# Expert layer: one region of rows per expert for the whole input, and finished tiles added to the result by an accumulating indirect DMA

## The reference

```python
# attention layer: Q, gate from layernorm(x); K, V from ctx (4 x 1024 x 512)
out = attn * gate @ Wo.T
x = x + out
# expert layer, on h = layernorm(x)
logits = einsum("bsd,de->bse", h, Wr)          # 8 experts
w, sel = top_k(logits, 2);  w = softmax(w)     # 2 experts per token, weights w
for e in range(8):
    out = out + gate[..., e:e+1] * (einsum("bsd,df->bsf", h, We[e]) + be[e])
x = x + out
```

## Time and profile before

| | us |
|---|---|
| median of three runs | 607.82 (605.88 to 607.92) |
| the profiled execution | 602.09 |
| its span, first to last instruction | 600.6 |
| TensorE busy in it | 546.1 |

### The profile page before, as it was taken

How to read it: one execution, slowest core, us unless ns; L and a number is a source line. 1 busy time by engine, 2 the same in 40 slices (tenths; PEclk the granted TensorE clock), 3 DMA queues, 4 the chain that set the end, 5 groups by cost and what they waited for, 6 DMA issues and landing times.

```text
span 600.6 us, 12872 instructions
## 1 busy us (share of the span) xinstructions
PE 546.1 (91%) x4192; PEld 443.6 (74%) x4193; DVE 320.0 (53%) x857; ACT 186.9 (31%) x340; POOL 166.9 (28%) x194
## 2 busy tenths in 40 slices
PE   6999996999999999999999999994899999999850
PEld 4778785788878888877888887883678888877630
DVE  4463374356436727535746645770566544447744
ACT  5456321334532343443244343231111111111100
POOL 3014645403633131554040350010112000055413
PEclk9999999799999999999999999996899999999995
DMA  8813344632453062355052137789847568789946
GB/s 270 308 37 106 141 141 169 201 122 108 149 196 114 18 229 71 139 179 207 4 202 80 72 141 297 264 286 420 306 147 241 145 206 269 226 254 369 408 178 189
DMA packets 44446, 114.18 MB, mean 190 GB/s; under 512 B 4976, under 2 KB 4976, under 8 KB 43504
## 3 DMA queue, kind: packets, MB, share of 16 engines
q1 hardware_dynamic: 24240, 57.43, 28.6%
q0 software_dynamic: 11232, 39.85, 18.5%
q10 hardware_dynamic: 8928, 16.26, 7.1%
HBM read 66.86 MB, written 46.66 MB: 189 GB/s over the span
## 4 chain that ended last, share of the span: by engine, by line
PE 61%; DMA 12%; issue 5%; POOL 3%; SPq 3%; DVE 3%; ACT 1%; POOLq 0%; DVEq 0%; ACTq 0%
PE pj L1098 17%; PE pj L1100 17%; PE pj L1099 17%; DMA khat<-xs 5%; PE tp L1090 4%; PE tp L1165 3%; DMA out_dram<-wraw 1%; DMA wraw<-in_L_ffn_We_dram 1%; POOL aux L533 1%; PE pj L1185 1%; PE kvb L1157 1%; DMA we_halves<-aux 1%; PE pj L1107 1%; DMA qhat<-y,gidx 1%; SPq L365 1%
## 5 line engine op out<-in xcount | busy, mean ns | idle before, releaser
L1098 PE MATMUL pj<-R 128*128 128x512 f32 x448 | 185.6, 414 | 10.3 <-DVE R L806 9.3
L1100 PE MATMUL pj<-R 128*128 128x512 f32 x448 | 177.4, 396 | 0.0
L1099 PE MATMUL pj<-R 128*128 128x512 f32 x448 | 176.8, 395 | 0.0
L1098 PEld LDWEIGHTS pj<-R 128*128 128x128 f32 x448 | 85.4, 191 | 27.4 <-DVE R L806 10.3
L1100 PEld LDWEIGHTS pj<-R 128*128 128x128 f32 x448 | 85.2, 190 | 19.3
L1099 PEld LDWEIGHTS pj<-R 128*128 128x128 f32 x448 | 85.7, 191 | 15.4
L1098 PE MATMUL pj<-R,aux 128*128 x184 | 77.5, 421 | 5.5 <-issue 3.6
L1100 PE MATMUL pj<-R,aux 128*128 x184 | 73.2, 398 | 0.0
L1099 PE MATMUL pj<-R,aux 128*128 x184 | 73.0, 397 | 0.0
L716 ACT CAST aux<-tp 128x512 fp32r<-128x512 f32 x46 | 26.9, 585 | 121.6 <-PE tp L1165 114.5
L806 DVE TENSOR_TENSOR R<-tp,R 128x512 fp32r<-128x512 f32 x64 | 43.8, 684 | 24.9 <-ACT R L638 24.7
(11 more groups left out here) (158 smaller groups left out, 652.5 us busy)
## 6 DMA issues: line engine op xcount, KB each, us to landing
we_halves<-aux POOLq DMA_DIRECT2D x14, 1024.0 KB, 5.0
R<-we_halves SPq DMA_DIRECT2D x7, 2048.0 KB, 11.9
khat<-xs SPq DMA_DIRECT2D x46, 256.0 KB, 3.6
wraw<-in_L_ffn_We_dram POOLq DMA_DIRECT2D x16, 512.0 KB, 6.4
buf<-in_ctx_dram SPq DMA_DIRECT2D x15, 512.0 KB, 3.8
y<-kvbd ACTq DMA_DIRECT2D x23, 256.0 KB, 3.6
y<-zeros ACTq DMA_DIRECT2D x23, 256.0 KB
wraw<-in_x_dram SPq DMA_DIRECT2D x4, 1024.0 KB, 8.0
```

Of the source, the lines that this page charges most:

```text
L1098: nc.tensor.matmul(bank[:, :], s_hi(k), m_hi(k), start=(k == 0), stop=False)
L1099: nc.tensor.matmul(bank[:, :], s_hi(k), m_lo(k), start=False, stop=False)
L1100: last = nc.tensor.matmul(bank[:, :], s_lo(k), m_hi(k), start=False, stop=(k == KT - 1))
```

## The change

There is one region of rows per expert for all four batches, and 39 tiles instead of 46. The first 17 are taken from the full tiles that the first three batches already give (`plan_full`), the other 22 from what is left when batch 3 is ranked (`plan_rest`). Each row in `xs` is 528 wide instead of 512: behind the normed row stand the token's weight for each expert, its number and a mark for rows that pad a tile. Rows and bias results have four buffers each instead of two.

A finished tile no longer goes to `y`. VectorE picks the weight and the number of each row's token (`pay`), adds the bias (`copy_y`), ScalarE multiplies by the weight (`scale_y`), and GpSimd adds the 128 rows to the result in device memory with one indirect DMA that accumulates (`add_rows`). Two tiles can hold the same token, and `add_rows(m)` waits until the add of tile m - 1 has landed. x2 is stored straight into the result. A pad row adds to the row of a token that is not otherwise in the tile; which one is worked out from the first 256 tokens (`mark_pads`, `find_pads`). The gathers, the combining on VectorE, the stores to `y` and of the result, and the loading of x2 are gone. All tiles stand in `START`, without loops.

The core of the diff:

```diff
-    GROUP_TILES = ((B - 1) * TT, TT)
-    ROWS = [n * P + P for n in GROUP_TILES]
...
+    ROWS = B * L + P
+    PAIRS = 2 * B * L
+    M0 = (2 * (B - 1) * L - E * (P - 1) + P - 1) // P
+    M_ALL = PAIRS // P + E - 1
+    M1 = M_ALL - M0
+    STEPS = B * L // P
...
+    XS, YS = 4, 4
...
+        for m in range(9, M_ALL):
+            START += tiles(m) + ([("C", "", 0)] if m == M0 - 2 else [])
+        START.remove(("T", "m", M_ALL))
...
+            def load_tile(m):
+
+                row = sp.value_load(tile_row[0:1, m:m + 1], min_val=0, max_val=E * ROWS)
+                if m >= XS:
+                    sp.wait_ge(MOE["t_m"], mth(m - XS))
+                    sp.wait_ge(paid, m - XS + 1)
+                sp.dma_start(xs_raw[:, m % XS, :], xs_dram[bass.ds(row, P), :]).then_inc(xs_loaded[m % XS], 16)
...
+                sp.wait_ge(wx_stored, 16 * 2 * e)
...
+            sp.wait_ge(SEMS["k"], nth("k", B - 1, ST - 1))
+            load_halves(1)
+            sp.wait_ge(SEMS["v"], nth("v", B - 1, ST - 1))
+            load_halves(2)
             sp.wait_ge(wx_stored, 16 * 2 * (E - 1))
-            sp.wait_ge(SEMS["v"], nth("v", B - 1, ST - 1))
-            load_halves(1)
-            load_halves(2)
+            sp.dma_start(be_all[:, 0:4, :], be[0:4, :].rearrange("(a e) d -> a e d", a=1).broadcast_to((P, 4, D))).then_inc(be_loaded, 16)
             sp.wait_ge(SEMS["q"], nth("q", B - 1, G - 1))
             load_halves(3)
+            sp.wait_ge(zeroed, 1)
+            sp.dma_start(xs_dram[E * ROWS:E * ROWS + P, :], zeros[:, :]).then_inc(padded, 16)
             sp.wait_ge(planned, 1)
-            sp.wait_ge(zeroed, 1)
-            with sp.Fori(0, E) as e:
-                pad(0, e, zeros[:, :])
-            sp.wait_ge(padded[0], 16 * E)
             for t in range(TT):
                 sp.wait_ge(scattered[t], 32 * (B - 1))
-            load_tile(0, 0, 0)
-            load_tile(0, 1, 1)
-            sp.wait_ge(SEMS["qhat"], nth("qhat", B - 1, G - 1))
-            for e in range(E):
-                sp.dma_start(be_all[:, e, :], be[e:e + 1, :].broadcast_to((P, D))).then_inc(be_loaded, 16)
+            for m in range(XS):
+                load_tile(m)
             sp.wait_ge(SEMS["g"], nth("g", B - 1, TT - 1))
             load_halves(4)
             load_halves(5)
-            load_tile(0, 2, 0)
+            load_tile(XS)
+            store_x2(B - 1)
             sp.wait_ge(SEMS["wo"], nth("wo", B - 1, TT - 1))
-            load_tile(0, 3, 1)
             load_halves(6)
-            load_tile(0, 4, 0)
+            load_tile(XS + 1)
             load_halves(7)
-            sp.wait_ge(x2_stored, 16 * B)
-            sp.wait_ge(SEMS["x2"], nth("x2", B - 1, TT - 1))
-            load_x2r(4, 4, x2r_loaded[1])
-            with sp.Fori(1, PAIRS - 4) as h:
-                load_tile(0, 2 * h + 3, 1)
-                load_tile(0, 2 * h + 4, 0)
+            for m in range(XS + 2, 14):
+                load_tile(m)
             sp.wait_ge(planned, 2)
-            sp.wait_ge(zeroed, 2)
-            for m in range(FIRST[1] - E, FIRST[1]):
-                load_tile(0, m, m % 2)
-                e = m - (FIRST[1] - E)
-                pad(1, e, bias[:, :])
-                if e >= 4:
-                    load_x2r(e - 4, 1, x2r_loaded[0])
-            sp.wait_ge(padded[1], 16 * E)
+            for e in range(E):
+                row = sp.value_load(pad_row[0:1, e:e + 1], min_val=0, max_val=E * ROWS - P)
+                sp.dma_start(xs_dram[bass.ds(row, P), :], zeros[:, :]).then_inc(padded, 16)
+            for m in range(14, M0):
+                load_tile(m)
+            sp.wait_ge(padded, 16 * (E + 1))
             for t in range(TT):
                 sp.wait_ge(scattered[t], 32 * B)
-            for m in range(FIRST[1], LOOP2):
-                load_tile(1, m, m % 2)
-            with sp.Fori(0, 3) as h:
-                for s in range(2):
-                    load_tile(1, 2 * h + LOOP2 + s, s)
-            for m in range(LOOP2 + 6, M_ALL):
-                load_tile(1, m, m % 2)
-                c = m - LOOP2 + 2
...
+            def add_rows(m):
+
+                slot = m % YS
+                if m == 0:
+                    pool.wait_ge(x2_stored, 16 * B)
+                if m == M0:
+                    pool.wait_ge(x2_stored, 16 * B + 16)
+                pool.wait_ge(y_scaled, m + 1)
+                if m >= 1:
+                    pool.wait_ge(added[(m - 1) % YS], 16 * ((m - 1) // YS + 1))
                 passed()
-                for j in range(2):
-                    nc.gpsimd.indirect_dma_start(out=yg[slot][j], out_offset=None, in_=y_dram[g][:, :],
-                                                 in_offset=bass.IndirectOffsetOnAxis(ap=gidx[:, slot, j:j + 1], axis=0)).then_inc(gathered[slot], 16)
-
-            def y_ready(g):
-
-                n = FIRST[g] + TILES[g]
-                pool.wait_ge(y_stored[0], 16 + 16 * ((n + 1) // 2))
-                pool.wait_ge(y_stored[1], 16 + 16 * (n // 2))
-
-            for t in range(TT):
-                pool.wait_ge(scattered[t], 32 * B)
-            y_ready(0)
-            with pool.Fori(0, N_COMB // 4) as h:
-                for s in range(4):
-                    gather(0, 4 * h + s, s)
-            y_ready(1)
-            for c in range(N_COMB, NQ):
-                gather(1, c, c % 4)
+                nc.gpsimd.indirect_dma_start(out=out_rows[:, :], out_offset=bass.IndirectOffsetOnAxis(ap=out_idx[:, m % (2 * YS):m % (2 * YS) + 1], axis=0),
+                                             in_=y_sb[slot], in_offset=None, compute_op=ALU.add).then_inc(added[slot], 16)
+
+            for step, kind, i in START:
+                if step == "M":
+                    if i >= 2:
+                        add_rows(i - 2)
+                elif step == "K":
+                    scatter(last, i)
+            add_rows(M_ALL - 2)
+            add_rows(M_ALL - 1)
+            for s in range(YS):
+                pool.wait_ge(added[s], 16 * ((M_ALL - 1 - s) // YS + 1))
...
+            def scale_y(m):
+
                 act.wait_ge(MOE["y_copied"], mth(m))
-                act.dma_start(y_dram[g][bass.ds((m - FIRST[g]) * P, P), :], y_sb[slot]).then_inc(y_stored[slot], 16)
-
-            def store_out(c, slot, res):
-                act.wait_ge(combined, c + 5)
-                act.dma_start(out_rows[bass.ds(c * P, P), :], res).then_inc(out_stored[slot], 16)
+                nc.scalar.activation(y_sb[m % YS], y_sb[m % YS], ACT.Identity, scale=w_sel[:, m % (2 * YS):m % (2 * YS) + 1]).then_inc(y_scaled, 1)
...
+                        act.dma_start(be_all[:, 4:8, :], be[4:8, :].rearrange("(a e) d -> a e d", a=1).broadcast_to((P, 4, D))).then_inc(be_loaded, 16)
...
-                q = bass.ds(b * TT + t, 1)
+                link(nc.vector.tensor_scalar(gate_1[:, :], both[:, t % 2, 0, :], w_top[:, 0:1], None, ALU.mult))
+                nc.vector.scalar_tensor_tensor(rows[t][:, GATES:GATES + E], both[:, t % 2, 1, :], w_top[:, 1:2], gate_1[:, :], ALU.mult, ALU.add)
+                nc.vector.tensor_scalar(rows[t][:, TOKEN:TOKEN + 1], rows[t][:, TOKEN:TOKEN + 1], float(L), None, ALU.add)
...
+            def copy_y(m):
+
                 dve.wait_ge(MOE["m_done"], mth(m))
-                dve.wait_ge(y_stored[slot], 16 * n + 16)
-                nc.vector.tensor_tensor(y_sb[slot], pj[slot][:, :], be_all[:, bass.ds(e, 1), :].rearrange("p a d -> p (a d)"), ALU.add).then_inc(MOE["y_copied"], 1)
-
-            def combine(c, slot, n, res, following=True):
...
+            def pay(m):
+
+                e = dve.value_load(tile_expert[0:1, m:m + 1], min_val=0, max_val=E - 1)
+                chosen[m] = e
+                n = m % (2 * YS)
+                row = xs_raw[:, m % XS, :]
+                nc.vector.tensor_scalar(w_sel[:, n:n + 1], row[:, bass.ds(e + GATES, 1)], 1.0, None, ALU.mult)
+                nc.vector.scalar_tensor_tensor(out_idx[:, n:n + 1], pad_token[:, bass.ds(e, 1)], row[:, PADDED:PADDED + 1], row[:, TOKEN:TOKEN + 1],
+                                               ALU.mult, ALU.add).then_inc(paid, 1)
+
```

More of the change, by code:

```diff
@@ L111, in xattn_moe_kernel @@
         w_raw += [gate[:, :, :], qhat[:, :, :], w_raw[0]]
[L112 to L118, removed]
+        normed = sb("normed", [P, 2, W])
+        rows = [normed[:, 0, :], normed[:, 1, :], num[:, 0, :], num[:, 1, :]]
+        xn = [r[:, 0:D] for r in rows]
         ident = sb("ident", [P, P])
@@ L143, in xattn_moe_kernel @@
         idf = sb("idf", [P, TT, E])
-        both = sb("both", [P, 2, E])
+        both = sb("both", [P, 2, 2, E])
+        gate_1 = sb("gate_1", [P, E])
+        early = sb("early", [P, 2, E])
+        early_members = sb("early_members", [P, 2, E], BF16)
+        early_run = sb("early_run", [P, E])
+        member_place = sb("member_place", [P, 2, E])
+        list_place = sb("list_place", [P, 2, E])
+        pad_token = sb("pad_token", [P, E])
         members = sb("members", [P, 2, E], BF16)
@@ L179, in xattn_moe_kernel @@
```

(21 more changed lines are left out.)

365 lines of the change are left out of this document (158 added, 207 removed).

## The result

The changed kernel takes 668.57 us (median of 4 runs, 666.99 to 670.28) against 607.87 us for the kernel before on the same chip (4 runs, 605.88 to 609.63). The ratio is 1.099, with a 95% interval of 1.097 to 1.102: it is slower by 61 us, where 21 were forecast. (All ratios here leave out the few executions in which the core was in a slower state, and can differ by up to 0.005 from the quotient of the two medians.) The profiled execution has a span of 667.2 us, 66.6 more than before.

The account below looks back on a forecast made before the run. TensorE bounds the kernel before; after the change the chain of adds does: 427.3 + 39 x 4.2 + 38 x 0.8 = 621.5 us span, plus 1.5 and 5.7 us offsets, rounded to 629; range 588 to 682.

Parts of the forecast that it names:

- first add starts: On GpSimd, after the last cut matrix lands at 426.5 us: the chain's first add starts at 427.3.
- wake-up, 38 times: Between an add's landing and the next add's issue on GpSimd: 0.8 us each, read from trace rows.
- the first term of the chain: An add's time from issue to landing: 4.2 us, as median scatter 3.3 plus 0.9 for reading the destination.
- The bounds of 2.7 and 6.6: Limits for an add's landing, in us: a plain scatter below, a gather and then a scatter above.
- within 1 us of the landing of the last add: End of the kernel, a sign to check: the span ends that close to the last add's landing.
- its last matmul would come near 539: End of the tile stage if TensorE still set the end: 577.9 - 22.3 - 6.4 - 10 us.
- rival A: Chain of adds: an add costs a scatter and one more reading, 3.4 us; 597.5 us, faster by 1.7%; chance 0.23.
- TensorE is busy for less than 520 us: Whole kernel, a sign to check: TensorE's busy time after the change, from 546.1 us before.
- Rival C: Tile stage: idling keeps TensorE's clock low, tiles take 6.1 us and are the bound; 646 us; chance 0.06.
- rival D: Chain of adds: the terms meet at the break-even landing of 3.67 us and nothing is seen; chance 0.06.
- Rival B: Chain of adds: reading and writing the destination follow one another entirely, 5.65 us per add; 685 us; chance 0.15.
- The Trainium skill's estimate: One GpSimd DMA: 2.0 us plus bytes over 436 GB/s; 2.6 us for 262 KB, 3.2 for an add.

Follow-up runs that it names:

- x10_calm: The changed kernel without the loads of rows from tile 14 on, so adds go to wrong tokens: 653.44 us, ratio 1.095.
- x2_none: The changed kernel with the adds' DMA left out and its semaphore raised at once, experts missing from the result: 573.07 us, ratio 0.941.
- x1_write: The changed kernel with each add made a plain write by the same indirect DMA, all waits kept: 596.99 us, ratio 0.980.
- x4_half: The changed kernel with each add taking 256 of 512 columns, into a buffer of its own: 629.54 us, ratio 1.050.
- x3_two: The changed kernel with adds alternating between two buffers, each waiting for the add two before, second buffer never merged: 584.25 us, ratio 0.959.
- x9_merge: The changed kernel with two add buffers merged at the end, SyncE's end wait, pad stores and bias wait moved; nothing left out: 589.11 us, ratio 0.983.
- x5_same: The changed kernel with adds of one expert allowed to overlap, waiting only at expert changes and padding tiles: 614.25 us, ratio 1.011.
- x11_halfwrite: The changed kernel with each add made a plain write of 256 of 512 columns into its own buffer: 578.81 us, ratio 0.966.
- x6_end: The changed kernel with the wait for the last four adds moved from GpSimd to SyncE: 666.46 us, ratio 1.111.
- x8_better: The changed kernel with adds overlapping within an expert, end wait on SyncE, pad stores on ScalarE's queue, later bias wait: 601.44 us, ratio 1.007.

## Why the prediction came out as it did

The direction and the mechanism were right, the size was not: 629 forecast, 669 measured. The chain of 39 adds is the bound, and its account by the prediction's own terms is this.

| term | forecast | trace after | effect on the span |
|---|---|---|---|
| first add starts | 427.3 | 425.10 | -2.2 |
| landing, 39 times | 4.2 | 5.28 | +42.1 |
| wake-up, 38 times | 0.8 | 0.81 | +0.4 |
| after the last landing | 0 | 5.4 | +5.4 |
| span | 621.5 | 667.2 | +45.7 |

(Landing and wake-up are means over all adds in the trace's semaphore records, from one add's start to the last of its 16 increments and from there to the next start.) The forecast time had another 7.2 us over the span, 1.5 and 5.7; after, the median is only 1.4 above the span, so 5.8 us of the error of the span are hidden in the comparison of 629 with 669.

- **The step that failed** is the first term of the chain: "I take the median scatter, 3.3, since loads of rows run beside the adds, plus 0.9 for reading the destination first: 0.6 for 262 KB at the 421 GB/s of the earlier trace rows and 0.3 for the later start of the write". It has two parts. The traffic, 0.5 to 0.6 in the 3.3, was right (0.5 to 0.6 by `x10_calm`). The 0.9 for accumulating should have been 2.0: 0.6 for a longer instruction, which the sum did not have at all, and 1.4 for longer work on the queues instead of 0.6 + 0.3. The bounds of 2.7 and 6.6 held it, and 3.3 + 2.0 gives the measured 5.3. Between ends so far apart the value was taken from the wrong side: the second DMA pass was priced as bytes at full rate, while in the traces an add goes out in twice as many packets as a write, smaller and slower per byte.
- The wake-up of 0.8, from one row of VectorE to GpSimd, held to 0.01 us over 38 waits (0.78 in most).
- The start held to 2.2 us: GpSimd does pass on the cut matrices first, and its first add has waited 22.08 us for `R<-we_halves`.
- **Not seen: the end.** "The landing of the last add, which is the end of the span" left out GpSimd's own drain, 4.9 us. In the kernel before it runs beside the combining, so the chain of the earlier trace rows doesn't show it. The sign "within 1 us of the landing of the last add" failed by this: 5.4 us.
- "If TensorE still set the end, its last matmul would come near 539" was wrong by some 25 us (`x2_none`, whose last matmul ends near 564): it took the waits for rows as gone and did not look at what is late next, the bias and SyncE's eight pad stores. This had no effect on 629, as the chain covers both, but it would have on rival A.
- "TensorE is busy for less than 520 us" was wrong: 542.6. Seven tiles are gone, but in the tile stage the granted clock is 0.82 to 0.90 of full speed, where it was 1.00 before, so part of the matmuls run at 1.2 GHz. Rival C was half right. The clock fell after TensorE began to idle between tiles, but it still idles 18.5 to 24.3 us in each of the three windows from 466 to 640 us, so the adds keep the pace. That the clock alone does not hold the tiles is shown by `x2_none`: without the adds it is 0.88 to 1.00 from 425 us on.
- Rival A, an add for the price of a write and one more reading, is excluded: 4.7 to 4.8 undisturbed for 3.4, and rival D with it, as a loss of 10% is plainly seen. `x1_write` shows its other half, though: with landings of 2.7 to 3.0 the change is a gain of 2%. With the 5.4 us of the end the break-even landing is (600.6 - 5.4 - 425.1 + 0.81) / 39 - 0.81 = 3.57 us; `x4_half`, at 4.0, is on the slow side of it as it should be.
- Rival B, everything twice in sequence with one instruction, had 5.65. It is nearer in number (685) than in mechanism: undisturbed the add is at 4.7.
- The Trainium skill's estimate (DMA: Bandwidth & Descriptors, section Anatomy of one DMA) holds for the write: 2.6 for 2.7 measured. For an add, with the bytes doubled, it gives 3.2, and the runs show 4.7 to 4.8. The Trainium skill's statement that a reducing DMA is slower for its two source reads and not for the addition (Collectives: The Full Stack, section on the bandwidth ceiling) can't be tested here, as no run has the second reading without the addition. What failed is the price put on that reading: on the queues an add takes 1.4 us more than a write, where 262 KB at 421 GB/s are 0.6, and GpSimd's instruction, which the sentence does not speak of, takes another 0.6.

## What to carry to other kernels

A read-modify-write DMA that must wait for the one before it is priced by its latency, not by its bytes at full rate: here 4.7 us alone, 5.3 with traffic, and 0.8 for the wait, against 3.2 us of compute per tile. Take the order away before making the add cheaper: two accumulators halve the chain (`x3_two`, 84.5 us of span less) for the price of one merge (`x9_merge`, 26 us). When an operation is not in the trace, bound the instruction that issues it and its packets apart, and ask at the end which engine's closing work has lost its cover.

## What the hardware showed that I had not expected

- The accumulating indirect DMA takes GpSimd 1549 or 1550 ns to issue, the writing one 954 to 957, with 512 columns or 256.
- The add goes out in 128 packets of one row each, the full write in 64 of two rows. In the trace's records one of the add's takes 178 ns on its queue for 2048 bytes, one of the write's 160 ns for 4096. At 178 ns each, 8 per engine, they would explain 1.4 of the 2.0 us that an add occupies the queues. The rest, 0.55 us, is in a few long ones: of the 128 packets of an add some 22 take 0.3 to 1.2 us (`x10_calm`, 600 to 645 us), while no packet of a write takes over 0.16 (`x1_write`, 569 to 591). Why they take so long stays open.
- The first packet of an add starts 2.12 us after its instruction does, that of a write 1.53 us: the longer instruction delays the data by all of its 0.6 us.
- GpSimd's drain takes 4889 ns after its last wait in the changed kernel, `x1_write`, `x3_two`, `x4_half`, `x5_same`, `x10_calm` and `x11_halfwrite`, and 5134 in `x2_none`. Where it begins with DMAs of GpSimd still in flight, it lasts until 2.2 to 2.6 us after the last of them has landed, whatever its length: 12042 ns in the kernel before, 7342 in `x6_end`, 7457 in `x8_better` and 24500 in `x9_merge`.
- Four accumulating DMAs of 1 MB from one buffer in device memory to another landed after 8.4 to 21.4 us, 4 MB in some 23 us.
